# Biases added as sums on GpSimd instead of matmuls, norms applied by ScalarE, presets on GpSimd, loads in pieces, and a new order of steps

## The chip, the cores and the metric

One NeuronCore of a Trainium2 chip runs the kernel alone. The metric is the device time of one launch in microseconds. TensorE (PE), VectorE (DVE), ScalarE (ACT) and GpSimd (POOL) each work through their own instruction list in order; SyncE (SP) only issues DMAs and waits. The engines meet by semaphores.

## The reference, cut to what matters

Four batches of 256 tokens with 128 channels, x, and as many context tokens. Five attention phases with 16 heads of 8 run one after the other, with a norm between them and one MLP after the third:

```
# phase 0: x = x + attend(rope(x Wq + bq), rope(ctx Wk), ctx Wv + bv) Wo + bo
# phase 1: per half h of the tokens (128 each), gates g from c = ctx[:, 0:2]
mod = silu(c) @ ada_w + ada_b        # nine shifts, scales and gates
x_h = x_h + g_msa[h] * mha(mod(ln(x_h)))
# phase 2: the halves attend to each other
x   = x + g_mca * (attend(q_h, k_other, v_other) @ crs_proj_w + crs_proj_b)
x_h = x_h + g_mlp[h] * (gelu(mod(ln(x_h)) @ fc1 + b1) @ fc2 + b2)
# phase 3: x = ln(attend(x, ctx) Wo.T + bo + x) * gamma + beta
# phase 4: x = x + attend(ln(x) * g + b, ctx), weights quantised to three values, + bo
```

## The kernel before, in words

`ORDER` is a written-out list of 1979 two-letter steps (a stream letter and a batch number). `make_steps` turns it into steps (kind, phase p, batch b, index i), and `streams` gives the engine of each stream. Every engine's program is the subsequence of `ORDER` with its steps, so the order is fixed by hand tables; `BANK_OF` gives the PSUM bank of each matmul step and `COUPLED` marks pairs of row steps (max or score) whose matmuls alternate on PE.

One phase of one batch: PE projects k, q and v (L731, L741, in phase 0 L720 and L721). ACT takes q and k with their bias to f32 (L876). POOL splits each into three bf16 parts (L597, L490, L492, L494; in phase 0 partly DVE). SP places each part into `q_stack` and `k_stack` with DMAs (L483), six for q and six for k. Both stacks are preset once per batch by DVE (L945, L946), batch 0's before the loop, the others by step `preset`. In phase 0 the positions are read, turned into row numbers on DVE, and POOL gathers the cosines and sines with indirect DMAs (L569); PE transposes them (L633), ACT takes them (L897), DVE rotates k and q (L991 to L996), and `add_turned` (L501) adds the two halves. PE multiplies the stacks for the row maxima (L662), DVE reduces them (L978), POOL splits the maxima (L507, L508), PE transposes them, ACT or DVE takes them (L900, L513), and SP places them as further rows of `q_stack` (L544). Then PE multiplies the scores with the maximum already subtracted (L663), ACT takes the exp (L844), PE multiplies by v (L705, in phases 1 and 2 L698), and ACT copies the heads out (L894). PE transposes (`unstack`, L633), DVE normalises (L1006, L1007), PE transposes (`heads_t`), ACT adds the bias of v (L903), and PE projects (`out_proj`, L800).

The biases of the output projection are matmuls: two per projection (L789), a column of the identity spread over 128 columns against a row of biases, `rows` in phases 0, 3 and 4, or `gated_bias` (gate times bias, formed by DVE in `take_gate`) in phases 1 and 2. They open the accumulation group that L800 closes. Each f32 matmul is two records in the profile. fc2's bias is made the same way (L816). `add_out` (L1021) adds x on DVE. Norms: DVE takes the statistics (L1030, L1033), POOL forms 1/deviation (L575, L576) and applies the norm (L518, two instructions per batch), PE transposes the result (`norm_t`) and ACT takes it with shift and scale (L914). In phase 3 there are two norms in a row, the first with gamma and beta on POOL (L624, L625).

ACT issues x, the bias rows and three weight groups in five DMAs (`load`; the group q1 to fc2d is one of 1 MB), stores the gates to DRAM and reads them back spread over 128 partitions in one DMA (`spread`, L862). POOL folds a gate into the output weights of phases 1 and 2 (`gate_fold`, L617).

## Time and profile before

| what | us |
|---|---|
| median of 3 runs | 316.98 |
| lowest, highest | 316.63, 322.85 |
| the profiled execution | 320.48 |
| its span | 318.6 |
| PE, DVE, ACT, POOL busy in it | 279.7, 228.2, 216.4, 185.7 |

The span goes from the first to the last instruction of the profiled execution; 1.9 us of its time lie around it. An engine's busy time is the union of its instructions. The chain is followed back from the last instruction, at each step to what released it. PE's instructions overlap each other, so that the busy time of a group can be longer than what it adds to the chain. A DMA's row in the timeline is its issue; its landing is a row of the chain.

### The profile page before, as it was taken

How to read it: one execution, taken by the hardware profiler on the slowest of the kernel's cores; microseconds unless marked ns; L12 is line 12 of the kernel's file. 1: busy time of each engine (PE TensorE's matmuls, PEld its weight loads, DVE VectorE, ACT ScalarE, POOL GpSimd, SP SyncE). 2: the span in 40 equal slices, each digit the busy share in tenths (PEclk: the TensorE clock that was granted, in tenths of full speed). 3: DMA queues.
4: the chain of work that ended last, by engine and by line, in shares of the span. 5: the costliest groups of instructions: out<-in, count | busy, mean ns of one | idle time of the engine just before them, and what ended most of it. 6: DMA issues, size and time to landing. Idle time of an engine off the chain costs nothing.

```text
span 318.6 us, 9133 instructions
## 1 busy us (share of the span) xinstructions
PE 279.7 (88%) x3268; PEld 173.6 (54%) x3268; DVE 228.2 (72%) x473; ACT 216.4 (68%) x462; POOL 185.7 (58%) x349
## 2 busy tenths in 40 slices
PE   2576688999979999988998999899999989999996
PEld 1462344465554666665676686657564546435535
DVE  4898859978872682776472687694979898888733
ACT  1023158668866768667788758898968786788972
POOL 3717414454764668787586759662879787851100
PEclk9977579999995999999999999999999999999999
DMA  4548911421382203333213212220123121220002
GB/s 132 149 110 254 289 24 35 110 59 37 92 245 67 72 26 80 99 84 83 71 45 84 52 52 54 52 69 10 44 61 77 37 67 44 72 74 23 3 3 66
DMA packets 40644, 24.75 MB, mean 78 GB/s; under 512 B 4880, under 2 KB 39576, under 8 KB 40344
## 3 DMA queue, kind: packets, MB, share of 16 engines
q1 hardware_dynamic: 37144, 17.71, 22.0%
q10 hardware_dynamic: 3072, 5.41, 5.2%
q0 software_dynamic: 384, 1.05, 1.1%
q8 instruction: 27, 0.44, 0.6%
q14 instruction: 17, 0.14, 0.2%
HBM read 7.56 MB, written 0.54 MB: 25 GB/s over the span
## 4 chain that ended last, share of the span: by engine, by line
PE 48%; DVE 12%; SPq 10%; DMA 10%; POOL 7%; issue 6%; ACT 5%; ACTq 1%; POOLq 0%; DVEq 0%
PE ps L705 9%; SPq L483 9%; PE ps L663 8%; PE ps L662 8%; PE ps L633 6%; DVE neg_max L978 5%; DMA q_stack<-max_rows_split 4%; PE ps L731 3%; PE ps L698 3%; PE ps L789 3%; DMA q_stack<-q_parts 2%; PE ps L800 2%; DVE k_stack L946 2%; PE ps L819 2%; ACT probs L844 2%
## 5 line engine op out<-in xcount | busy, mean ns | idle before, releaser
L978 DVE TENSOR_REDUCE neg_max<-ps 128x2 f32<-128x512 f32 (+1 forms) x256 | 160.0, 682 | 36.3 <-PE ps L662 35.8
L844 ACT ACTIVATE probs<-ps 128x512 f32<-128x512 f32 x256 | 134.4, 605 | 29.2 <-PE ps L663 26.8
L662 PE MATMUL ps<-k_stack,q_stack 62*128 62x256 bf16 (+1 forms) x640 | 62.9, 259 | 9.8 <-DMA q_stack<-q_parts 5.9
L663 PE MATMUL ps<-q_stack,k_stack 64*128 64x256 bf16 (+1 forms) x640 | 58.8, 254 | 10.2 <-DMA q_stack<-max_rows_split 5.9
L705 PE MATMUL ps<-probs,v_cols 128*32 128x256 f32 x768 | 55.3, 394 | 0.3 <-ACT probs L844 0.2
L662 PEld LDWEIGHTS ps<-k_stack,q_stack 62*128 62x128 bf16 x640 | 28.9, 96 | 39.6 <-issue 10.3
L663 PEld LDWEIGHTS ps<-q_stack,k_stack 64*128 64x128 bf16 x640 | 29.4, 95 | 32.6 <-DMA q_stack<-max_rows_split 8.8
L705 PEld LDWEIGHTS ps<-probs,v_cols 128*32 128x32 f32 x768 | 20.4, 110 | 17.6 <-issue 8.8
L507 POOL CAST max_parts<-neg_max 128x16 bf16<-128x16 f32 (+2 forms) x34 | 6.8, 200 | 39.2 <-DVE neg_max L978 38.7
L876 ACT ACTIVATE q_f<-ps,vec 128x256 f32<-128x256 f32 x32 | 15.0, 476 | 8.2 <-PE ps L731 8.0
L894 ACT ACTIVATE heads_raw<-ps 128x512 f32<-128x512 f32 x20 | 12.0, 600 | 12.6 <-PE ps L705 7.8
L518 POOL TENSOR_SCALAR heads_normed<-x,mean_var,rstd 128x128 f32<-128x128 f32 x24 | 18.9, 798 | 1.3
L698 PE MATMUL ps<-probs,v_cols 128*32 128x128 f32 x512 | 19.1, 277 | 0.0
L1006 DVE RECIPROCAL inv_sum<-ps 128x32 f32<-128x32 f32 x20 | 7.0, 349 | 16.5 <-PE ps L633 16.5
L575 POOL TENSOR_SCALAR var_eps<-mean_var 128x2 f32<-128x2 f32 x20 | 4.6, 228 | 22.0 <-DVE mean_var L1033 21.4
L490 POOL TENSOR_TENSOR q_parts<-q_f,q_parts 128x256 bf16<-128x256 f32 x19 | 12.7, 670 | 6.9 <-ACT q_parts L870 5.9
L731 PE MATMUL ps<-src_t,w 128*128 128x256 f32 x48 | 15.8, 425 | 0.9 <-ACT src_t L914 0.6
L633 PE MATMUL ps<-ident_f,heads_normed 128*128 128x128 f32 x72 | 14.7, 290 | 1.0 <-POOL heads_normed L518 0.3
L576 POOL TENSOR_TENSOR rstd<-var_eps,minus_half 128x2 f32<-128x2 f32 x20 | 14.4, 719 | 1.7
L903 ACT ACTIVATE heads_t_gated<-ps,vec 128x256 f32<-128x256 f32 x20 | 9.2, 472 | 7.9 <-PE ps L633 7.9
L698 PEld LDWEIGHTS ps<-probs,v_cols 128*32 128x32 f32 x512 | 12.6, 109 | 3.1 <-ACT probs L844 1.0
L597 POOL CAST q_parts<-q_f 128x256 bf16<-128x256 f32 x16 | 6.3, 396 | 12.8 <-ACT q_f L876 12.8
(123 smaller groups left out, 451.5 us busy)
## 6 DMA issues: line engine op xcount, KB each, us to landing
k_stack<-k_parts SPq DMA_DIRECT2D x120, 64.0 KB, 2.1
q_stack<-q_parts SPq DMA_DIRECT2D x114, 64.0 KB, 2.1
gates<-gates_dram ACTq DMA_DIRECT2D x1, 1536.0 KB, 7.1
w<-in_w ACTq DMA_DIRECT2D x1, 1024.0 KB, 9.7
rows<-in_rows ACTq DMA_DIRECT2D x1, 704.0 KB, 6.0
q_stack<-max_rows_split SPq DMA_DIRECT2D x44, 4.0 KB
w<-in_w ACTq DMA_DIRECT2D x1, 576.0 KB, 7.1
ctx_t<-in_ctx_t SPq DMA_DIRECT2D x4, 128.0 KB, 2.9
```

Of the source, the lines that this page charges most:

```text
L483: queue.dma_start(stack[slot::ROW_SLOTS, b, :, :], parts_of(kind, b)[part]).then_inc(sem_, 16)
L518: last = ops.tensor_scalar(heads_normed[:, b, qt, :], src[:, b, qt, :], mean_var[:, b, qt, 0:1], rstd[:, b, qt:qt + 1], ALU.subtract, ALU. ...
L576: link(nc.gpsimd.tensor_tensor(rstd[:, b, :], var_eps[:, b, :], minus_half[:, :], ALU.pow))
L633: return nc.tensor.transpose(out, src, by)
L662: return nc.tensor.matmul(out, queries, keys, start=True, stop=True)
L663: return nc.tensor.matmul(out, keys, queries, start=True, stop=True)
L698: last = nc.tensor.matmul(ps[BANKS - 1][32 * j:32 * j + 32, g * T + at * P:g * T + (at + 1) * P], v_cols[:, b, keys_tile(p, at), h, :], pr ...
L705: last = nc.tensor.matmul(ps[BANKS - 1][32 * j:32 * j + 32, g * T:(g + 1) * T], v_cols[:, b, at, h, :], pr[:, at * T:(at + 1) * T], start= ...
L731: last = nc.tensor.matmul(out[:, 0:T], W(f"{kind}{p}"), src[:, b, :], start=True, stop=True)
L844: nc.scalar.activation(probs[:, n % PROB_BUFS, :], ps[bank_of["score", p, b, i]][:, :], ACT.Exp, scale=SCALE).then_inc(of(st), 1)
L876: nc.scalar.activation(f, src, ACT.Identity, bias=V(f"b{letter}{p}")).then_inc(of(st), 1)
L978: nc.vector.tensor_reduce(dst, src, AX.X, ALU.max, negate=True).then_inc(of(st), 1)
```

## The change

The two bias matmuls of every output projection and of fc2 are gone, and each projection is its own accumulation group. POOL forms `base` = x + bias (or x + gate x bias) with a new step `base` per phase and batch and `base_mlp` before the MLP's sum, and DVE's `add_out` and `add_mlp` add `base` instead of x. `gate_fold` now also forms gate x bias, in place for phases 1 and 2 and as `gate_bias` for the MLP, so there are 12 folds instead of 8, the first 8 with two products. The 16 norms that feed `norm_t` are applied by ACT as (1/deviation) x + shift; POOL's new step `deviation` computes the shift with two more small instructions. The presets are on POOL, seen as f32 (half as many elements), batch 0's ahead of the wait for the positions. Seven loads instead of five: the 1 MB group is cut in three. The spread is cut in four, one semaphore per batch. `ORDER` (2028 steps), `BANK_OF` and `COUPLED` are written anew. The ORDER of POOL begins with gathers 1 and 2, then presets 2 and 1. A second copy of the branches `base` and `base_mlp` is never reached and is left out below, as are the tables.

```diff
-APPLY_ON = ("pool", "pool", "pool", "pool")
+PART_ON = ("act", "pool", "pool", "pool", "pool")
+APPLY_ON = ("act", "act", "act", "act")
...
+LOADS = ("x", "rows", 2, 1, 3, 4, 5)
+SPREADS = B
+W_GROUP = (0, 1, 3, 5, 5)
...
-        "Y": ("dve", only([("preset", 0, 0)], not first)),
+        "Y": ("pool", only([("preset", 0, 0)], not first)),
...
-        "p": ("dve", [("apply", p, 1) for p in phases[:-1] if APPLY_ON[p] == "dve"]),
+        "p": ("pool", [("deviation", p, 1) for p in phases[:-1] if APPLY_ON[p] == "act"]),
...
+        "b": ("pool", [("base", p, 0) for p in phases]),
+        "B": ("pool", [("base_mlp", 2, 0)]),
+        "Z": ("pool", [("gate_fold", i, 0) for i in range(3)]),
...
-        "4": ("act", only([("spread", 0, 0), ("spread", 0, 1)], first)),
-        "9": ("act", only([("load", 0, i) for i in range(5)], first)),
+        "4": ("act", only([("keep_gates", 0, 0)] + [("spread", 0, i) for i in range(SPREADS)], first)),
+        "9": ("act", only([("load", 0, i) for i in range(len(LOADS))], first)),
...
-W_GROUPS = (("v0", "o0"), ("q1", "fc2d"), ("ada0", "ada8"), ("q3", "o4"))
+W_GROUPS = (("v0", "o0"), ("q1", "o1"), ("ada0", "ada8"), ("q2", "o2"), ("fc1a", "fc2d"), ("q3", "o4"))
...
+        def preset_stacks(ops, b):
+            ops.memset(q_stack[:, b, :, :].rearrange("p e t -> p (e t)").bitcast(F32), 0.0)
+            return ops.memset(k_stack[:, b, :, :].rearrange("p e t -> p (e t)").bitcast(F32), TWO_ONES)
...
-                link(nc.gpsimd.tensor_tensor(rstd[:, b, :], var_eps[:, b, :], minus_half[:, :], ALU.pow))
+                return nc.gpsimd.tensor_tensor(rstd[:, b, :], var_eps[:, b, :], minus_half[:, :], ALU.pow)
 
             link(nc.gpsimd.memset(minus_half[:, :], -0.5))
             nc.gpsimd.memset(mean_mat[:, :], 1.0 / (D * D)).then_inc(mean_set, 1)
+            clear_v(FIRST[1]).then_inc(first_v_cleared, 1)
+            preset_stacks(nc.gpsimd, FIRST[1]).then_inc(first_preset, 1)
             pool.wait_ge(pos_ready, 1)
             gather(FIRST[1])
-            clear_v(FIRST[1]).then_inc(first_v_cleared, 1)
...
+                elif kind == "preset":
+                    preset_stacks(nc.gpsimd, b).then_inc(of(st), 1)
...
+                    pool.wait_ge(gates_spread[b], 16)
+                    pool.wait_ge(rows_loaded, 16)
+                    if p < 2:
+                        pool.wait_ge(w_loaded[W_GROUP[p + 1]], 16)
+                        pool.wait_ge(*done("rope", 0, b, 0))
+                        link(nc.gpsimd.tensor_tensor(rope_gated_o[:, 2 * b:2 * b + 2, p, :],
+                                                     w[:, W_AT[f"o{p + 1}"]:W_AT[f"o{p + 1}"] + 1, :].broadcast_to([P, NT, D]),
+                                                     gates[:, 2 * b:2 * b + 2, p, :], ALU.mult))
+                        g = gates[:, 2 * b:2 * b + 2, p, :]
+                        nc.gpsimd.tensor_tensor(g, g, row2(f"bo{p + 1}"), ALU.mult).then_inc(of(st), 1)
+                    else:
+                        nc.gpsimd.tensor_tensor(gate_bias[:, 2 * b:2 * b + 2, :], gates[:, 2 * b:2 * b + 2, 2, :],
+                                                row2("bfc2"), ALU.mult).then_inc(of(st), 1)
+                elif kind == "base":
+                    if p == 0:
+                        pool.wait_ge(x_loaded, 16)
+                        pool.wait_ge(rows_loaded, 16)
+                    elif p == 3:
+                        pool.wait_ge(mlp_added, mlp_no(b))
+                    elif p == 4:
+                        pool.wait_ge(*done("apply", 3, b, 0))
+                    else:
+                        pool.wait_ge(*done("add_out", p - 1, b, 0))
+                        pool.wait_ge(*done("gate_fold", p - 1, b, 0))
+                    add = gates[:, 2 * b:2 * b + 2, p - 1, :] if p in (1, 2) else row2({0: "bo0", 3: "bo3", 4: "bo4"}[p])
+                    nc.gpsimd.tensor_tensor(base[:, b, :, :], x[:, b, :, :], add, ALU.add).then_inc(of(st), 1)
+                elif kind == "base_mlp":
+                    pool.wait_ge(*done("add_out", p, b, 0))
+                    pool.wait_ge(*done("gate_fold", 2, b, 0))
+                    nc.gpsimd.tensor_tensor(base[:, b, :, :], x[:, b, :, :], gate_bias[:, 2 * b:2 * b + 2, :], ALU.add
+                                            ).then_inc(of(st), 1)
...
+                    pool.wait_ge(*done("base", p, b, 0))
+                    link(inverse_deviation(p, b, 0))
...
+                elif kind == "deviation":
+                    pool.wait_ge(*done("stats", p, b, int(p == 3)))
+                    nc.gpsimd.tensor_scalar(minus_mean[:, b, :], mean_var[:, b, :, 0], -1.0, None, ALU.mult)
+                    link(inverse_deviation(p, b, int(p == 3)))
+                    nc.gpsimd.tensor_tensor(shift[:, b, :], minus_mean[:, b, :], rstd[:, b, :], ALU.mult).then_inc(of(st), 1)
...
-                    pe.wait_ge(const_loaded, 16)
-                    pe.wait_ge(rows_loaded, 16)
-                    if p in (1, 2):
-                        pe.wait_ge(*done("take_gate", 0, 0, 0))
-                    for qt in range(NT):
-                        nc.tensor.matmul(out[:, qt * D:(qt + 1) * D], *bias_rows(b, qt, p), start=(qt == 0), stop=False,
-                                         skip_group_check=True)
...
-                                                start=False, stop=(qt == NT - 1), skip_group_check=True)
+                                                start=True, stop=True)
...
+                    pe.wait_ge(w_loaded[4], 16)
...
-                        nc.tensor.matmul(out[:, qt * D:(qt + 1) * D], ident[:, 0:1].broadcast_to([P, P]),
-                                         rows[:, R_AT["bfc2"], :], start=True, stop=False)
...
+                    load_w(act, LOADS[i])
+                elif kind == "keep_gates":
                     act.wait_ge(*done("take_gate", 0, 0, 0))
                     act.dma_start(gates_dram.rearrange("(r c) -> r c", r=2 * B),
                                   gates_small[:, :, :].rearrange("r k c -> r (k c)")).then_inc(gates_stored, 16)
...
-                    act.wait_ge(gates_stored, 16)
-                    act.dma_start(gates[:, :, :, :].rearrange("p r k c -> p (r k c)"), gates_dram.partition_broadcast(P)
-                                  ).then_inc(gates_spread, 16)
+                    if i == 0:
+                        act.wait_ge(gates_stored, 16)
+                    n = 2 * 3 * D
+                    act.dma_start(gates[:, 2 * i:2 * i + 2, :, :].rearrange("p r k c -> p (r k c)"),
+                                  gates_dram[n * i:n * (i + 1)].partition_broadcast(P)).then_inc(gates_spread[i], 16)
...
+                elif kind == "apply":
+                    act.wait_ge(*done("deviation", p, b, 1))
+                    src = (heads_t_gated if p == 1 else x)[:, b, :, :]
+                    for qt in range(NT):
+                        last = nc.scalar.activation(heads_normed[:, b, qt, :], src[:, qt, :], ACT.Identity,
+                                                    bias=shift[:, b, qt:qt + 1], scale=rstd[:, b, qt:qt + 1])
+                    last.then_inc(of(st), 1)
...
-            preset_stacks(FIRST[1], first_preset)
...
-                    if p == 0:
-                        dve.wait_ge(x_loaded, 16)
-                    elif p == 3:
-                        dve.wait_ge(mlp_added, mlp_no(b))
-                    elif p == 4:
-                        dve.wait_ge(*done("apply", 3, b, 0))
-                    else:
-                        dve.wait_ge(*done("add_out", 0, b, 0))
+                    dve.wait_ge(*done("base", p, b, 0))
...
-                                            x[:, b, :, :], ALU.add).then_inc(of(st), 1)
+                                            base[:, b, :, :], ALU.add).then_inc(of(st), 1)
...
+                    dve.wait_ge(*done("base_mlp", p, b, 0))
+                    dve.wait_ge(gates_spread[b], 16)
...
-                    nc.vector.tensor_tensor(x[:, b, :, :], product, x[:, b, :, :], ALU.add).then_inc(mlp_added, 1)
+                    nc.vector.tensor_tensor(x[:, b, :, :], product, base[:, b, :, :], ALU.add).then_inc(mlp_added, 1)
...
-                    nc.vector.memset(gated_bias[:, :, :], 0.0)
-                    link(nc.vector.tensor_tensor(gates_small[:, :, :],
-                                                 ps[bank_of["gate", 0, 0, 0]][0:2 * B, 0:3 * D].rearrange("p (a b) -> p a b", a=3),
-                                                 rows[0:2 * B, R_AT["gate1"]:R_AT["gate3"] + 1, :], ALU.add))
-                    nc.vector.tensor_tensor(gated_bias[0:2 * B, :, :], gates_small[:, 0:2, :],
-                                            rows[0:2 * B, R_AT["bo1"]:R_AT["bo2"] + 1, :], ALU.mult).then_inc(of(st), 1)
+                    nc.vector.tensor_tensor(gates_small[:, :, :],
+                                            ps[bank_of["gate", 0, 0, 0]][0:2 * B, 0:3 * D].rearrange("p (a b) -> p a b", a=3),
+                                            rows[0:2 * B, R_AT["gate1"]:R_AT["gate3"] + 1, :], ALU.add).then_inc(of(st), 1)
```

## Rows read from the trace of the kernel before

**Rows 1.** The page: busy time of each engine, share of the span, instructions.
```profile
PE 279.7 (88%) x3268; PEld 173.6 (54%) x3268; DVE 228.2 (72%) x473; ACT 216.4 (68%) x462; POOL 185.7 (58%) x349
```

**Rows 2.** The chain that ended last: shares by engine (the page), by line (the chain).
```profile
PE 48%; DVE 12%; SPq 10%; DMA 10%; POOL 7%; issue 6%; ACT 5%; ACTq 1%; POOLq 0%; DVEq 0%
...
by line: PE ps L705 9.1%; SPq L483 8.8%; PE ps L663 8.5%; PE ps L662 8.5%; PE ps L633 6.4%; issue 5.5%; DVE neg_max L978 5.4%; DMA q_stack<-max_rows_split 4.2%; PE ps L731 3.1%; PE ps L698 2.9%; PE ps L789 2.6%; DMA q_stack<-q_parts 2.2%; P
```

**Rows 3.** The page: TensorE's granted clock in 40 slices of 7.97 us.
```profile
PEclk9977579999995999999999999999999999999999
```

**Rows 4.** Timeline, 0 to 36 us: start, duration, engine, line, operation [idle before, releaser].
```profile
5.76 1.30 POOL L569 DMA_INDIRECT rope_gated_o<-in_rope,pos_row  x1 [4.68 <-DVE pos_row L954]
...
11.37 0.60 ACT L897 ACTIVATE rope_hidden<-ps 128x512 f32<-128x512 f32 x1 [6.97 <-PE ps L633]
...
14.62 1.76 DVE L946 MEMSET k_stack<- 128x2048 bf16 x1 [0.38 <-issue]
...
16.30 0.36 DVE L995 TENSOR_TENSOR q_f<-ps,rope_hidden 128x256 f32<-128x256 f32 x1
...
24.97 0.57 ACTq L849 DMA_DIRECT2D x<-in_x  x1
...
26.42 0.61 PE L662 MATMUL ps<-k_stack,q_stack 62*128 62x256 bf16 x6 [3.12 <-DMA q_stack<-q_parts]
```

**Rows 5.** Groups by line and form: count, busy us, mean ns, idle before.
```profile
L518 POOL TENSOR_SCALAR heads_normed<-x,mean_var,rstd 128x128 f32<-128x128 f32 x24 | 18.9, 798 | 1.3
...
L518 POOL TENSOR_SCALAR heads_normed<-heads_t_gated,mean_var,rstd 128x128 f32<-128x128 f32 x16 | 12.6, 798 | 0.8
...
L914 ACT ACTIVATE src_t<-ps,mods 128x128 f32<-128x128 f32 x24 | 9.8, 464 | 1.5 <-PE ps L633 1.4
...
L946 DVE MEMSET k_stack<- 128x2048 bf16 x4 | 7.1, 1765 | 1.5 <-issue 1.5
...
L617 POOL TENSOR_TENSOR rope_gated_o<-w,gates 128x256 f32<-128x256 f32 x8 | 5.8, 727 | 0.1
...
L575 POOL TENSOR_SCALAR var_eps<-mean_var 128x2 f32<-128x2 f32 x20 | 4.6, 228 | 22.0 <-DVE mean_var L1033 21.4 <-POOL q_parts L494 0.2
...
L561 POOL MEMSET v_cols<- 128x1024 f32 x4 | 3.8, 954 | 0.1
...
L945 DVE MEMSET q_stack<- 128x1024 uint32 x4 | 3.6, 912 | 0.6 <-issue 0.6
...
L564 POOL MEMSET v_cols<- 128x128 f32 x8 | 1.4, 204 | 0.2
```

**Rows 6.** Groups by line and form: the bias matmuls on TensorE.
```profile
L789 PE MATMUL ps<-rows,ident_f 128*128 128x128 f32 x48 | 8.1, 292 | 0.6 <-ACT heads_t_gated L903 0.6
...
L789 PE MATMUL ps<-gated_bias,ident_f 128*128 128x128 f32 x32 | 5.5, 294 | 0.3 <-ACT heads_t_gated L903 0.3
...
L816 PE MATMUL ps<-rows,ident_f 128*128 128x128 f32 x16 | 3.2, 281 | 0.0
```

**Rows 7.** The chain, 300 to 318.6 us: start, duration, what.
```profile
313.24 0.45 PE ps L789 x4
```

**Rows 8.** The chain at three max placements, and the page on the spread.
```profile
34.97 4.83 DMA q_stack<-max_rows_split
...
89.05 5.11 DMA q_stack<-max_rows_split
...
215.54 1.78 DMA q_stack<-max_rows_split
...
gates<-gates_dram ACTq DMA_DIRECT2D x1, 1536.0 KB, 7.1
```

**Rows 9.** The chain, 40 to 80 us: the fourth preset and take_gate.
```profile
55.45 1.76 DVE k_stack L946
...
73.17 0.77 DVE gated_bias L1058
```

**Rows 10.** The waits: engine, line, waited for: us in all, times, longest.
```profile
POOL var_eps L575 <- DVE mean_var L1033: 21.4, 12, 6.9
```

## What I expect of the change, and why

> **What bounds the kernel now.** I read the busy line first, then the slices, the chain, and last the stretches where the chain leaves TensorE. Busy: PE 279.7 us of a 318.6 us span, DVE 228.2, ACT 216.4, POOL 185.7 [rows 1]. TensorE is the nearest to a bound, but the chain that ended last lies on PE for only 48%: 12% is DVE, 10% SP's issuing, 10% DMA, 7% POOL, 5% ACT [rows 2]. So microseconds taken from PE count where the chain is on PE, and the rest must come from the waits. The clock row shows three places that are not steady: slices 3, 4 and 6 at 0.7, slice 5 (31.9 to 39.8 us) at 0.5, and slice 13 (95.6 to 103.5) at 0.5, i.e. 1.2 GHz instead of 2.4 [rows 3]. Everywhere else it is 0.9 or more. Each of the 0.5 slices holds or follows a long landing of a row-max placement [rows 8]. The three kinds of place where the change acts are thus: the start, two DMA stalls, and the bias matmuls spread over the whole.
>
> **1. Presets leave DVE.** Four pairs of memsets (L945, L946), 0.91 + 1.77 us each, 10.7 us of DVE in all [rows 5]. At the start, batch 0's cos/sin are in SBUF when L897 ends, 11.37 + 0.60 = 11.97 us. DVE is then still in presets, the last of which (L946 at 14.62) ends at 16.4, and the rotation of k (L995) begins at 16.30 [rows 4]. Without presets on DVE it begins at about 12.0: 4.3 us earlier. What follows down to the first max matmul at 26.42 [rows 4] is the same ladder of small DVE steps and placements (the new order has the same ones in nearly the same order, one turn later for batch 1), so it should come at about 22. The fourth pair lies in the chain at 54 to 57: 1.76 + 0.91 and the gap between them, 3.0 us [rows 9]. On POOL the pair is two memsets over 1024 f32 (the bitcast halves the element count): the row for that shape is 0.954 us, 1.9 a pair, 7.6 for all [rows 5]. For batch 0, v_cols (0.95 + 2 x 0.2) and the pair now stand ahead of the first gather, which started at 5.76 after 4.68 us in which POOL only waited for positions [rows 4]: POOL is free from 1.1 us, and 3.3 us of memsets [rows 5] end at about 4.5. They are covered; if POOL's own gaps use that up, the gather comes up to 0.5 us late and the whole start with it. The presets of batches 1 and 2 stand behind two gathers each of 2.6 us (each gather is two DMAs of 1.3 us; the presets end at about 17), in time for placements of batch 1 after 20. Terms: -4.3 (range -2 to -5) and -3.0 (0 to -3.0).
>
> **2. Bias matmuls go.** 20 output projections lose two f32 matmuls each (four records) and fc2 loses two for each of four batches: L789 8.1 + 5.5 us and L816 3.2 us of PE busy, 16.8 in all [rows 6]. That is busy time of pipelined instructions. In the tail, where projections stand back to back, a bias step advances the chain by 0.45 us [rows 7]. So 24 x 0.45 = 10.8 us of PE are freed. The chain itself has 2.6% of 318.6 = 8.3 us on L789 [rows 2]. Off the chain the freed time only becomes idle. I take -8 (range -3 to -10.8); the last four steps, 1.8 us in the tail, are certain.
> The Trainium skill ("Perfetto Trace Analysis", Identifying the Most-Contended Engine) says that matmul busy share is a poor measure because the instructions are pipelined. This trace agrees: 16.8 us busy against 10.8 advanced; by the busy figure the sum would be 6 us lower.
>
> **3. Sums, folds and norms.** POOL gets 20 base sums, 4 base_mlp and 12 more gate products of 128x256 f32, by the nearest row 0.727 each [rows 5]: 36 x 0.727 = 26.2. Deviation adds two 128x2 ops of 0.228 at 16 places: 7.3. Presets 7.6. It loses the 32 applies of i = 1 (of 24 + 16) at 0.798: 25.5 [rows 5]. Net +15.5, POOL at 201 us. The phases themselves are neutral (+0.73 + 0.46 - 1.6 = -0.4 per norm); the growth is presets and folds, most of it early, where POOL has room. POOL turns 22 of its 186 us into chain (7%) [rows 1, 2], 12%; I take +1.9 (0 to +8). The sum over x (base) is queued before its projection, needs only the previous residual, and lies under that phase's scores; if it were late, DVE's add_out and with it the bank would wait 0.7 us each. DVE's waits at add_out are the same count. take_gate loses a memset and a product, of which 0.77 is on the chain [rows 9]: -1.0 (0 to -1).
> ACT gets 32 applies of 128x128 with bias and scale from SBUF: nearest row L914, 9.8 / 24 = 0.41 [rows 5], 13.1 us (7 to 15), and five more DMA issues of 0.57 [rows 4], 2.9. ACT goes to about 232 us, still under PE's 263. In its queue the exps stand behind each apply, and PE's score banks wait for exps. ACT turns 16 of 216 us into chain (5%), 7%; but these sit behind a new wait (for deviation), so I take a quarter of 16: +4.0 (+1 to +16). Chain of one norm, L576 aside, which stays: 0.23 + 1.6 before, 3 x 0.23 + 0.8 and one more hop after: equal, 0.
>
> **4. Loads in pieces.** At 34.97 and 89.05 the placement of row maxima (4 KB) lands after 4.83 and 5.11 us; the same placement takes 1.78 at 215.54 [rows 8]. The first follows x, rows and two groups of weights, issued on ACT's queue from 24.97 on at about 0.6 us each [rows 4]; the second follows the gate spread, 1536 KB in one DMA that lands in 7.1 us [rows 8]. Now the spread goes in four parts of 384 KB and the big group in three, fc and phase 3 weights much later. Excess: 3.05 and 3.3 us. The first keeps most of its bytes in front (x, rows, ada stay), the second loses three quarters of them. I take the second, -3.3 (0 to -6.4), and nothing for the first. The clock of slice 13 fell right after this second pause: a gain on top that I don't count.
>
> **Sum.** -4.3 - 3.0 - 8.0 - 1.0 - 3.3 + 4.0 + 1.9 = -13.7 us against the profiled execution (320.5 us, span 318.6), so 306.8 there. The median of the runs is 317.0, 3.5 below it; scaled, -13.5: I predict 303.5 us. A change within 2% (310.6 to 323.3) is about what a measurement of this kernel cannot tell from none. The order of all steps is new as well, with the same number of exps and maxima ahead of each projection, 181 coupled row steps against 177, and the same nine switches between exp and gelu: no term for it, but it is what can move every term.
>
> **Rivals.**
> A. *The forecast*, 298 to 308: chance 0.47.
> B. *Everything lands*: all 10.8 of PE, both stalls (6.4), no ACT cost, and a clock that doesn't fall in slice 13. -4.3 - 3.0 - 10.8 - 1.0 - 6.4 + 1.9 = -23.6, about 293.5. For it: PE busy in nearly all slices. Against: 52% of the chain is elsewhere. Chance 0.11 (292 to 298).
> C. *Pieces change nothing in the landings, and DVE hides its presets*: the bytes are the same and the DMA engines are shared, the placement still waits 5 us behind them, and the fourth preset was hidden. -13.7 + 3.3 + 3.0 = -7.4, about 309.5 (308 to 311). For it: stall one keeps its bytes. Chance 0.17. The Trainium skill ("DMA: Bandwidth & Descriptors", Issuing engines are not separate DMA queues) says that DMAs of all engines interleave on the same 16 engines; by it alone only fewer bytes in front of a placement help, and the first landing here, on another queue than the loads, agrees.
> D. *The bound moves on*: DMA issue on SP (10% of the chain) and POOL's splits fill the freed time, only start and tail are left: -4.3 - 1.8 - 1.0 + 1.9 = -5.2 or less, 312 (311 to 317). For it: 0.6 us issues stand in the chain for 8.8% [rows 2]. Chance 0.18.
> E. *Slower: ACT parks behind POOL.* The apply waits in ACT's queue for deviation. POOL itself waited for statistics 21.4 us in 12 waits, 1.8 each [rows 10]. If ACT stands as long at each of 16 applies, with exps behind it, that is +28.5 in place of +4.0: 303.5 + 24.5 = 328. From 1.1 us each the gain is gone, from 1.5 it is over 2% slower. Against: a queue order can put exps ahead of the apply, and ACT has 32% of slack. Chance 0.07 (over 317), half of it over 323.
>
> Faster by over 2%: A, B and C but for their edge, 0.73; within 2%: 0.23; slower: 0.04. The range 295 to 312 leaves out E, most of D and the lower half of B.
>
> **What would show it.** Right: L995's counterpart at about 12 us and the first max at about 22; no memset on DVE; PE busy near 263; the landing after the first gate spread under 2.5 us; no 0.5 in slice 13; tail from last value matmul to the end 1.5 to 2 us shorter. Wrong: a gather after 6.2 us; ACT waits on deviation of over 15 us in all; exps' waits up while PE is idle between; POOL over 90% busy in the last third, with base late. If PE's busy falls by 16 and its idle time rises by as much, D is the case.

## The result, and the profile after

| kernel | median us | ratio to the kernel before | 95% interval |
|---|---|---|---|
| before | 319.15 | 1 | |
| changed | 303.63 | 0.9531 | 0.9427 to 0.9635 |
| predicted | 303.5 (295 to 312) | | |

Over all occasions on which it ran, the kernel before scatters from 316.4 to 328.7 us between its executions and the changed one from 299.2 to 304.2, so a ratio is known to about one per cent and no better. On two later occasions the changed kernel ran again beside others, at 300.6 and 301.2 us (ratios 0.9345 and 0.9448). Both kernels have a slower state, over 1.5% above the fastest execution, in some executions; ratios and intervals leave those out, medians keep them. The profiled execution went from a span of 318.6 to 302.1 us.

The page of the changed kernel (busy time, TensorE's granted clock in 40 slices, and the chain's shares by engine) answers [rows 1 to 3]:

```profile
PE 269.0 (89%) x3172; PEld 164.6 (54%) x3172; DVE 215.8 (71%) x463; ACT 225.0 (74%) x494; POOL 199.2 (66%) x393
...
PEclk9968799999999799799789999999999999999998
...
PE 60%; DMA 9%; DVE 8%; ACT 7%; POOL 6%; issue 6%; SPq 4%; ACTq 0%; POOLq 0%; DVEq 0%
```

In this execution the chain was on TensorE for 60% of 302.1 us (181 us), against 48% of 318.6 (153 us) before. One profile isn't enough for such a share. In the two later profiles of the same kernel it is 51% of 297.9 (152 us), whose line is below, and 54% of 298.5 (161 us):

```profile
PE 51%; POOL 12%; DMA 8%; DVE 8%; issue 7%; ACT 6%; SPq 6%; ACTq 0%; POOLq 0%
```

What all three show is less time of the chain elsewhere: 166 us before, and 121, 146 and 137 us now. SP's issuing went from 10% to 4, 6 and 4%, DVE from 12% to 8% in all three. GpSimd has 6, 12 and 11%, against 7% before. So the kernel got shorter because the chain spends less time off TensorE; whether it spends more on it differs from execution to execution.

The start in the timeline (start, duration, engine, line, operation, what ended the idle time), against [rows 4]:

```profile
2.32 0.95 POOL L506 MEMSET q_stack<- 128x1024 f32 x1
...
3.21 0.95 POOL L507 MEMSET k_stack<- 128x1024 f32 x1
...
5.97 1.31 POOL L581 DMA_INDIRECT rope_gated_o<-in_rope,pos_row  x1 [1.81 <-DVE pos_row L1020]
...
12.05 0.42 DVE L1060 TENSOR_TENSOR q_f<-ps,rope_hidden 128x256 f32<-128x256 f32 x1 [6.39 <-ACT rope_hidden L960]
...
23.52 0.98 PE L726 MATMUL ps<-k_stack,q_stack 62*128 62x256 bf16 x8 [1.41 <-DVE heads_normed L1061]
...
35.40 0.60 ACT L900 ACTIVATE probs<-ps 128x512 f32<-128x512 f32 x1 [0.78 <-PE ps L727]
```

GpSimd's presets end at 4.2 us, and it still waits 1.81 us for the positions; the rotation begins at 12.05 instead of 16.30; the first max (its matmuls) comes at 23.52 instead of 26.42 and the first exp at 35.40 instead of 40.49.

What was added, in the groups by line and form (count, busy us, mean ns, idle before), against [rows 5]:

```profile
L998 ACT ACTIVATE heads_normed<-x,shift,rstd 128x128 f32<-128x128 f32 x24 | 10.5, 484 | 1.6 <-POOL shift L692 1.6
...
L654 POOL TENSOR_TENSOR base<-x,rows 128x256 f32<-128x256 f32 x12 | 8.5, 725 | 0.7 <-DVE x L1099 0.7
...
L638 POOL TENSOR_TENSOR gates<-gates,rows 128x256 f32<-128x256 f32 x8 | 5.8, 725 | 0.6
...
L690 POOL TENSOR_SCALAR minus_mean<-mean_var 128x2 f32<-128x2 f32 x16 | 3.9, 242 | 14.6 <-DVE mean_var L1089 14.3
...
L506 POOL MEMSET q_stack<- 128x1024 f32 x4 | 3.9, 962 | 0.1
```

And a stall that the kernel before did not have, in the timeline from 140 us:

```profile
140.41 1.37 SPq L556 DMA_DIRECT2D q_stack<-max_rows  x2
...
140.42 0.34 ACTq L472 DMA_DIRECT2D w<-in_w  x1
...
140.80 0.45 ACTq L472 DMA_DIRECT2D w<-in_w  x1
```

in the chain of waits (start, duration, what):

```profile
141.13 5.07 DMA q_stack<-max_rows
```

and in the windows around it (length, then busy us and instructions of PE, PEld, DVE, ACT and POOL, granted clock, DMA share, GB/s):

```profile
140.00:147.00 7.00, 2.62 (x33) 1.95 (x32) 1.85 (x7) 1.76 (x4) 6.30 (x12) 0.99 0.58 186
147.00:153.00 6.00, 5.79 (x68) 3.89 (x66) 3.22 (x9) 3.73 (x9) 1.22 (x3) 0.50 0.00 0
```

Two weight loads of 512 KB are issued in the same microsecond as a placement of row maxima (8 KB). The placement lands after 5.07 us, TensorE is busy for 2.62 of 7 us, and it then runs at a granted clock of 0.50, the 1.2 GHz level, for the next six. The stall of [rows 8] at 89 us is gone, and this one has taken its place.

### The profile page after: what moved, and what is told of

Same layout as the page of the kernel before. It is cut to its first block, busy times and chain, and to the rows that moved or that the text cites. A ratio compares the mean times of both kernels' runs of the same rounds, so it can differ in the third digit from the quotient of the medians.

```text
span 302.1 us, 9011 instructions
## 1 busy us (share of the span) xinstructions
PE 269.0 (89%) x3172; PEld 164.6 (54%) x3172; DVE 215.8 (71%) x463; ACT 225.0 (74%) x494; POOL 199.2 (66%) x393
## 4 chain that ended last, share of the span: by engine, by line
PE 60%; DMA 9%; DVE 8%; ACT 7%; POOL 6%; issue 6%; SPq 4%; ACTq 0%; POOLq 0%; DVEq 0%
PE ps L769 11%; PE ps L726 11%; PE ps L727 9%; PE ps L697 9%; PE ps L795 4%; DVE neg_max L1043 4%; PE ps L857 3%; PE ps L762 3%; ACT probs L900 3%; DMA q_stack<-q_parts 3%; PE ps L875 3%; SPq L491 2%; PE ps L805 2%; DMA q_stack<-max_rows 2%; PE ps L868 1%
## 5 line engine op out<-in xcount | busy, mean ns | idle before, releaser
L727 PE MATMUL ps<-q_stack,k_stack 64*128 64x256 bf16 (+1 forms) x640 | 60.2, 253 | 4.9 <-DMA q_stack<-max_rows 3.6
L769 PE MATMUL ps<-probs,v_cols 128*32 128x256 f32 x768 | 53.5, 386 | 0.5 <-ACT probs L900 0.5
L726 PEld LDWEIGHTS ps<-k_stack,q_stack 62*128 62x128 bf16 x640 | 30.7, 97 | 33.2 <-issue 10.7
L762 PE MATMUL ps<-probs,v_cols 128*32 128x128 f32 x512 | 20.3, 286 | 0.6 <-ACT probs L900 0.6
L1077 DVE TENSOR_TENSOR x<-ps,base 128x256 f32<-128x256 f32 x12 | 5.0, 422 | 15.4 <-PE ps L857 15.1
L502 POOL TENSOR_TENSOR q_parts<-split_r,q_parts 128x256 bf16<-128x256 f32 x19 | 12.7, 670 | 1.5
L498 POOL TENSOR_TENSOR k_parts<-q_f,k_parts 128x256 bf16<-128x256 f32 x18 | 12.1, 670 | 2.4 <-ACT k_parts L928 1.6
L697 PE MATMUL ps<-ident_f,heads_raw 128*128 128x128 f32 x80 | 13.3, 290 | 0.5 <-ACT heads_raw L957 0.5
L690 POOL TENSOR_SCALAR minus_mean<-mean_var 128x2 f32<-128x2 f32 x16 | 3.9, 242 | 14.6 <-DVE mean_var L1089 14.3
```

The costliest lines, as they stand in the source:

```text
L498: ops.tensor_tensor(part[1], full, part[0], ALU.subtract).then_inc(of(step), 1)
L502: ops.tensor_tensor(part[2], rest, part[1], ALU.subtract).then_inc(of(step), 1)
L697: return nc.tensor.transpose(out, src, by)
L726: return nc.tensor.matmul(out, queries, keys, start=True, stop=True)
L727: return nc.tensor.matmul(out, keys, queries, start=True, stop=True)
L762: last = nc.tensor.matmul(ps[BANKS - 1][32 * j:32 * j + 32, g * T + at * P:g * T + (at + 1) * P], v_cols[:, b, keys_tile(p, at), h, :], pr ...
```

## The experiments

Each is the changed kernel with one thing altered (4, 5 and 6 alter several), beside the kernel before on the same chip. Ratios are to the kernel before. Runs 1 to 3 had the first yardstick on their chip, runs 5, 6 and the second of 9 the other; runs 4, 7, 8 and the first of 9 had none, and are set against the three ratios of the changed kernel.

**The yardsticks.** The changed kernel ran twice more, with no edit.

> The changed kernel unchanged, as the yardstick on this chip for the other runs of the call. Every theory: 0.953 of the kernel before, about 303.6 us, within 1%.

> The changed kernel unchanged, the yardstick of this call. Every theory: 0.935 to 0.953 of the kernel before, about 300 to 304 us.

Measured: 300.56 us, 0.9345 (0.9254 to 0.9436), and 301.24 us, 0.9448 (0.9367 to 0.9529). TensorE's busy time was 263.4 and 263.2 us in their profiles, against 269.0 in the one above, at a mean clock of 0.971 and 0.976 against 0.952.

**1. Presets back on VectorE.**

```diff
-        "Y": ("pool", only([("preset", 0, 0)], not first)),
+        "Y": ("dve", only([("preset", 0, 0)], not first)),
...
-            preset_stacks(nc.gpsimd, FIRST[1]).then_inc(first_preset, 1)
...
+            preset_dve(FIRST[1]).then_inc(first_preset, 1)
```

> The changed kernel, with all four preset pairs back on VectorE in the order that the kernel before has them (batch 0's before the loop, the others at their place in the new order, bf16 as before). Theory (the presets on VectorE held up the start by 4.3 us and lay in the chain with 3.0 us later): 5 to 7 us slower than the changed kernel, the first rotation of k no earlier than 14 us, against 12.05 now. Rival (VectorE has slack, the presets are hidden, or only the place in the order matters): less than 2 us slower.

Measured: 311.37 us, 0.9642 (0.9537 to 0.9747), 10.8 us slower than the yardstick of the same chip. The rotation still began at 11.96 us: batch 0's preset was over before the rotation could start, and the two others stand behind the first rotations in the new order. They hit the splits instead. The timeline (same columns as above):

```profile
17.48 0.91 DVE L1012 MEMSET q_stack<- 128x1024 uint32 x1 [0.16 <-issue]
18.77 1.76 DVE L1013 MEMSET k_stack<- 128x2048 bf16 x1 [0.38 <-issue]
...
20.70 0.91 DVE L1012 MEMSET q_stack<- 128x1024 uint32 x1 [0.16 <-issue]
...
21.99 1.76 DVE L1013 MEMSET k_stack<- 128x2048 bf16 x1 [0.38 <-issue]
...
29.16 1.19 PE L723 MATMUL ps<-k_stack,q_stack 62*128 62x256 bf16 x8 [8.96 <-DVE heads_normed L1063]
```

The first max came at 29.16 us after TensorE had stood for 8.96 us; in the changed kernel's profile above, at 23.52 after 1.41, and in the yardstick's from the same chip at 21.64 after 2.12. So 7.5 of the 10.8 us are there. Presets on VectorE do hold the start, by more than was expected, though not at the rotation: what was expected of the place was wrong, of the mechanism right. The edit brings back two things together, the engine and the bf16 form of k_stack's preset (1.76 us, where q_stack's 32-bit form takes 0.91 for the same bytes). What 32-bit presets on VectorE would cost was not run.

**2. The bias matmuls back, the sums kept.**

```diff
                 elif kind == "out_proj":
+                    for qt in range(NT):
+                        nc.tensor.matmul(out[:, qt * D:(qt + 1) * D], ident[:, 0:1].broadcast_to([P, P]), zero_row[:, :],
+                                         start=(qt == 0), stop=False, skip_group_check=True)
...
                 elif kind == "fc2":
...
+                        nc.tensor.matmul(out[:, qt * D:(qt + 1) * D], ident[:, 0:1].broadcast_to([P, P]), zero_row[:, :],
+                                         start=True, stop=False)
```

> The changed kernel, with the two bias matmuls of every output projection and of fc2 put back on TensorE at their old places in the program, with a row of zeros, while the sums on GpSimd stay: the pure price of 48 f32 matmuls. Theory: 8 us slower than the changed kernel (3 to 10.8), TensorE busy up by 16 us. Rival (the freed time was idle time anyway, the bound is on the other engines): under 3 us slower, with TensorE's idle time falling by as much as its busy time grows.

Measured: 310.78 us, 0.9611 (0.9516 to 0.9705), 10.2 us slower. TensorE was busy 278.5 us at a mean granted clock of 0.949, 15.1 more than in the yardstick (263.4 at 0.971), but only 9.5 more than in the first profile (269.0 at 0.952), whose clock is nearer. The groups of the zero-row matmuls:

```profile
L852 PE MATMUL ps<-zero_row,ident_f 128*128 128x128 f32 x80 | 14.1, 301 | 1.5 <-ACT heads_t_gated L974 1.4
...
L880 PE MATMUL ps<-zero_row,ident_f 128*128 128x128 f32 x16 | 3.3, 290 | 0.2 <-ACT rope_hidden L999 0.2
```

That is 17.4 us of busy time, for steps that advance a chain by 0.45 us each, 10.8 in all [rows 7]. Nearly all of the 10.8 came back as time. In the new order TensorE's freed time is not idle.

**3. Norms applied on GpSimd.**

```diff
                 elif kind == "deviation":
-                    nc.gpsimd.tensor_scalar(minus_mean[:, b, :], mean_var[:, b, :, 0], -1.0, None, ALU.mult)
                     link(inverse_deviation(p, b, int(p == 3)))
-                    nc.gpsimd.tensor_tensor(shift[:, b, :], minus_mean[:, b, :], rstd[:, b, :], ALU.mult).then_inc(of(st), 1)
+                    apply_norm(nc.gpsimd, b, heads_t_gated if p == 1 else x).then_inc(of(st), 1)
...
-                    act.wait_ge(*done("deviation", p, b, 1))
-                    src = (heads_t_gated if p == 1 else x)[:, b, :, :]
-                    for qt in range(NT):
-                        last = nc.scalar.activation(heads_normed[:, b, qt, :], src[:, qt, :], ACT.Identity,
-                                                    bias=shift[:, b, qt:qt + 1], scale=rstd[:, b, qt:qt + 1])
```

> The changed kernel, with the 16 norms that feed the transposes applied by GpSimd again, at the place of the deviation step; ScalarE's 32 activations and the two small deviation steps are gone. Theory of the prediction (ScalarE pays 4 us for the applies and issues, GpSimd 1.9 for all its extra work; undoing saves ScalarE 13 us and loads GpSimd with 18): within 3 us either way, ScalarE about 211 us busy, GpSimd about 217. Rival (GpSimd is the engine that is short in this order): 4 us or more slower, with the waits for parts and for the maxima's split growing.

Measured: 310.04 us, 0.9588 (0.9494 to 0.9682), 9.5 us slower: the rival. The page, of this run's execution of 314.42 us (mean granted clock 0.929): busy time, the chain's shares by engine, and by line:

```profile
PE 274.0 (88%) x3172; PEld 166.6 (53%) x3172; DVE 216.1 (69%) x463; ACT 214.5 (69%) x462; POOL 217.6 (70%) x393
...
PE 38%; POOL 20%; DVE 13%; DMA 10%; issue 8%; SPq 7%; ACT 3%; POOLq 0%; ACTq 0%; DVEq 0%
PE ps L768 8%; PE ps L725 7%; DVE neg_max L1037 7%; DMA q_stack<-q_parts 6%; PE ps L696 6%; PE ps L726 5%; SPq L491 5%; POOL heads_normed L530 5%; PE ps L794 3%; PE ps L761 2%; POOL rstd L588 2%; PE ps L856 2%; PE ps L874 2%; POOL q_parts L498 2%; SPq L556 1%
```

GpSimd at 70% busy is on the chain for 20% of the span, where the changed kernel has it at 66 or 67% busy and, in its three profiles, 6, 12 and 11% of the chain. An engine that is far from full can still be the one that holds the chain. Added up along the chain, the applies (L530) stand in it for 15 us, against 1.6 in each profile of the changed kernel, and the splits of q and k, which stand in GpSimd's queue behind them, for 26 us against 7. This chain is of one execution, the longest of the four; the 9.5 us are between the medians.

**4. All parts in the old order.** The three tables `ORDER`, `BANK_OF` and `COUPLED` are those of the kernel before, with the new steps set in by a rule: presets after gather 2, each base before its normalise and after its fold, deviation in the apply's old place, ScalarE's apply right before norm_t, the third fold and base_mlp after add_out of phase 2. First lines of `ORDER`:

```diff
-    "K0K1I1Q0R0z0r0D0r0k0K2D010R1y0z1r1q0D1Q300k1I2Y2R2Y1E0y010E0Q1r1Q2W1y110J2D10000I311y1z2r2r2d2901111q121d2q2W2w2"
...
+    "K0R0z0r0Q0r0K1I1R1z1D0D0k0Q1q0I2Y2Y110R2z2r1y0E0r100I300E000y0W01010D1D1k19090Q2W190K2r2d2r2J1y1909090M0M0M0m0m0"
...
```

> All parts of the change (sums on GpSimd, norms on ScalarE, presets on GpSimd, loads and spread in pieces), but with the order, bank and coupling tables of the kernel before; the new steps are put in by rule: a preset after the gather, the sum ahead of the normalisation of its phase, the apply ahead of its transpose, the three loads together at the fourth load's place, the four spreads together at the second spread's. Theory of the prediction (no term for the order): within 3 us of the changed kernel. Rival (the new order earns a good part of the gain, because each part has its own best place): 5 us or more slower than the changed kernel, though faster than the kernel before.

Measured: 331.31 us, 1.0335 (1.0235 to 1.0435): slower than the kernel before, though every part is in. The waits of TensorE, in its execution of 335.27 us, name one cause (engine, tile, line, what it waited for: us, times, longest):

```profile
PE ps L697 <- ACT heads_normed L998: 18.5, 14, 1.7
```

and in the changed kernel the same row is

```profile
PE ps L697 <- ACT heads_normed L998: 1.0, 2, 0.9
```

The transposes waited for an apply that stood in ScalarE's queue, where the rule puts it right ahead of them; the apply itself waited for GpSimd's shift for only 0.5 us in all. That is a bad place that my rule chose, so the next run takes it away.

**5. The same, norms on GpSimd.** The edits of 3 and 4 together. On top of 4:

```diff
-                    nc.gpsimd.tensor_tensor(shift[:, b, :], minus_mean[:, b, :], rstd[:, b, :], ALU.mult).then_inc(of(st), 1)
+                    apply_norm(nc.gpsimd, b, heads_t_gated if p == 1 else x).then_inc(of(st), 1)
```

> The old order with the new parts by rule, as in the earlier run, but with the norms applied by GpSimd, so that no transpose waits for an apply in ScalarE's queue (18.5 us of TensorE's waits there). If the bad place of the apply was the whole loss: below the kernel before by 4% or so, near 305 us. If the old order cannot use any of the parts: still 315 us or more. In between, the difference to the changed kernel with the apply on GpSimd (310.0) is the worth of the order alone.

Measured: 321.47 us, 1.0103 (1.0023 to 1.0182), the kernel before being at 321.05. Without the waits for the apply, presets off VectorE, no bias matmuls and smaller loads bring nothing in the old order, where my rule puts them. The applies on ScalarE cost 2.3% there (1.0103 against 1.0335) and save 2.4% in the new order (0.9588 against 0.9345).

This run also settles a question on the loads. The spread is in four parts, but issued together (81.14 to 83.27 us), and the placement of row maxima behind them still lands late, as in the kernel before (5.11 us at 89.05):

```profile
84.59 5.09 DMA q_stack<-max_rows_split
```

In run 4 the same placement takes 6.29 us. So cutting the spread in pieces does not remove that stall by itself.

**6. The new order with the old parts.** Edits 1, 2 and 3, the one-piece spread of 7, and no sums (the edit of 8) together. The bias is left out of the result. The seven loads stay.

```diff
+        "Y": ("dve", only([("preset", 0, 0)], not first)),
...
+                    apply_norm(nc.gpsimd, b, heads_t_gated if p == 1 else x).then_inc(of(st), 1)
...
+                        nc.tensor.matmul(out[:, qt * D:(qt + 1) * D], ident[:, 0:1].broadcast_to([P, P]), zero_row[:, :],
...
-                    nc.gpsimd.tensor_tensor(base[:, b, :, :], x[:, b, :, :], add, ALU.add).then_inc(of(st), 1)
```

> The new order with the old parts: presets on VectorE, norms applied on GpSimd, 48 bias matmuls on TensorE (of a row of zeros), no sums or bias products on GpSimd, the spread in one DMA. The bias is left out of the result, its work is there. If the parts bring what they brought one at a time (10.8 + 10.2 + 9.5 us, less what the sums cost GpSimd) and add up: 325 us or more, slower than the kernel before. If the order brings the gain and the parts share one gain among them: 308 to 315 us.

Measured: 326.7 us, 1.0253 (1.019 to 1.0316), against 301.24 for the changed kernel beside it: 25.5 us. One at a time the parts were worth 10.8 + 10.2 + 9.5 = 30.5 us; so in the new order they nearly add up. This kernel has no sums on GpSimd, so their cost is not in the 25.5.

**7. The gate spread in one DMA.**

```diff
                         act.wait_ge(gates_stored, 16)
-                    n = 2 * 3 * D
-                    act.dma_start(gates[:, 2 * i:2 * i + 2, :, :].rearrange("p r k c -> p (r k c)"),
-                                  gates_dram[n * i:n * (i + 1)].partition_broadcast(P)).then_inc(gates_spread[i], 16)
+                        act.dma_start(gates[:, :, :, :].rearrange("p r k c -> p (r k c)"),
+                                      gates_dram.partition_broadcast(P)).then_inc(gates_spread[0], 16)
```

> The changed kernel with the gate spread in one DMA of 1536 KB at the place of the first of the four. Theory (the single spread stood in front of a placement of row maxima, 3.3 us): 2 to 5 us slower, with a landing of 4 us or more between 64 and 75 us. Rival (the bytes are the same, and at this place of the new order nothing urgent is behind them): within 1.5 us of the changed kernel.

Measured: 303.95 us, 0.9491 (0.9409 to 0.9573), inside the span of the changed kernel's three ratios, so no difference that these runs resolve. Its chain has this row:

```profile
65.17 8.77 DMA gates<-gates_dram
```

One spread lands after 8.77 us, where the four land after 3.8 to 5.2 each, and the chain does wait for it (the first fold needs it). It did not delay a placement of row maxima: the next one is issued only at 73.76 us. Whether that is worth one or two microseconds stays open.

**8. No sums and no bias products on GpSimd.** The biases of the output projections and of fc2 are left out of the computation.

```diff
-                    nc.gpsimd.tensor_tensor(base[:, b, :, :], x[:, b, :, :], add, ALU.add).then_inc(of(st), 1)
...
-                        nc.gpsimd.tensor_tensor(g, g, row2(f"bo{p + 1}"), ALU.mult).then_inc(of(st), 1)
...
-                                            base[:, b, :, :], ALU.add).then_inc(of(st), 1)
+                                            x[:, b, :, :], ALU.add).then_inc(of(st), 1)
```

> The changed kernel without any bias in the output projections and fc2: the 24 sums and the 12 bias products on GpSimd are left out (36 instructions of 0.73 us, 26 us of GpSimd), and VectorE adds x as before. Theory of the prediction (GpSimd turns 12% of its work into the chain): 2 to 4 us faster than the changed kernel. Rival (GpSimd is the engine that is short): 6 us or more faster. A third: equal, because the sums lie where GpSimd waits anyway.

Measured: 301.17 us, 0.9412 (0.9323 to 0.95), again among the changed kernel's own ratios. 25.6 us of GpSimd's work went (busy 174.5 instead of 200.1), and its wait for the statistics grew from 14.3 us to this:

```profile
POOL minus_mean L652 <- DVE mean_var L1058: 25.1, 12, 7.1
```

A good part of the sums, 11 of 26 us by this row, lies where GpSimd would wait anyway. 18 us more of applies cost 9.5 us (run 3), and 26 us of sums no more than these runs resolve: 1 us by the mean of the changed kernel's three ratios (0.9441), some 4 at the edge of the intervals. What I take from it, that the work differs in whether something waits behind it, fits the chain of run 3.

**9. The two late loads moved away from the placement.**

In `ORDER`, the two steps written `90` that stood side by side, at 901 and 902 of 2028, now stand at 230 and 281, where the trace has about 48 and 54 us:

```diff
-    "V0h0U3t3229090U0n0U3U0t0S1S1S1e1S1S1M2b0o3x3p3S1U0o0e1V1e1V1M2M2M2m2e1V1m2m2x0v3m2V1e1S1S1e1e1e1N3u3M2m2M2M2m2m2"
...
+    "31S1S1e1S1M290i3M2m2m2e1U0t0S1e1S1S1U0V1V1e1e1e1S1S1e1e1S1S1b0o0x0e1e1M2m2M2m213V1V1j3j3M2S1S1m2M2m2G0e1M2S1p0S1"
+    "M2902323s2e1e1T2g0V123M2M2M2C2m2m2m2m2M2V1e1V1v0b2m2N0u0V1h1G013m2W032g0M2w0S2e2S2b3m2b1s2e2M3U140Q0q070K0T2C232"
...
```

> The changed kernel with the two 512 KB weight loads, which ScalarE now issues at 140.4 us in the same moment as a placement of row maxima that then lands after 5.07 us, moved to about 48 and 54 us. Theory (a load in front of an urgent placement costs its landing and the slower clock after it): 3 to 6 us faster than the changed kernel, TensorE's busy share between 140 and 147 us back above 0.8 and no stretch at the 1.2 GHz level behind it. Rival (another placement near 50 us waits instead, or the placement at 140 is slow for another reason): within 1.5 us.

> The changed kernel with the two late weight loads moved to about 48 and 54 us, a second time beside the changed kernel on one chip. Theory: 3 to 6 us faster than the changed kernel of the same call. Rival (the difference between calls was that of the chips): within 1.5 us.

Measured: 298.01 us, 0.9256 (0.9136 to 0.9376), and 298.15 us, 0.9347 (0.9264 to 0.9429), the second beside 301.24 for the changed kernel on the same chip (0.9448). The windows of the changed kernel in its last run:

```profile
136.00:142.00 6.00, 4.26 (x78) 3.07 (x68) 2.94 (x10) 3.19 (x7) 4.81 (x9) 1.00 0.61 164
142.00:148.00 6.00, 3.65 (x48) 3.00 (x48) 0.56 (x2) 3.10 (x7) 3.48 (x8) 0.72 0.27 93
```

and of this kernel beside it:

```profile
136.00:142.00 6.00, 4.99 (x94) 3.74 (x90) 3.30 (x9) 3.49 (x8) 4.08 (x8) 1.00 0.27 70
142.00:148.00 6.00, 5.32 (x115) 3.99 (x118) 3.95 (x13) 5.55 (x12) 5.18 (x11) 1.00 0.05 14
```

The stall and the low clock behind it are gone: TensorE waits for that placement for 0.31 us, where it waited for 3.37 in the first profile. Another transfer into q_stack, near the loads' new place, now takes 2.86 us (its row in the chain):

```profile
48.88 2.86 DMA q_stack<-max_rows_split
```

The profiled spans are 298.5 and 295.7. This is the fastest kernel of the study, by about 3 us or 1%; the intervals of the two ratios overlap, and on the first yardstick's chip the changed kernel itself had 0.9345. So the sign rests on two measurements and on the trace together, and the size is at the low end of what was expected.

## Why the prediction was right, and where its steps were not

The total was 303.5 against 303.63. It is right in that TensorE's matmuls and the start gained, and in the size, but two of its terms were too small, one had the wrong sign, and the order had no term. They cancelled: part of the closeness is luck, and on two later occasions the same kernel took 300.6 and 301.2 us.

- **Presets, -7.3.** The start moved as told: rotation at 12.05 (12.0 told), gather not late, first max at 23.52, in the yardsticks' profiles from about 22 (22 told). Undoing it costs 10.8 in the new order. The term was too small for that order, because I counted only DVE's own time; TensorE also stood for 8.96 us before the first max. Not told either: in the two yardsticks' profiles the chain of the first 25 us runs over GpSimd, through the gathers and the presets of batches 2 and 1 (3.6 us), so the presets are not covered there.
- **Bias matmuls, -8.0 (3 to 10.8).** Undoing them costs 10.2, close to the upper bound, 24 x 0.45. I had cut the sum to what lay on the chain of the kernel before (8.3 us). That chain had 52% elsewhere, and that share was 40, 49 and 46% in the profiles of the changed kernel. PE busy "near 263" was 269.0 in the profile shown and 263.4 and 263.2 in the others: busy time of matmuls moves with the granted clock. The Trainium skill ("Perfetto Trace Analysis", Identifying the Most-Contended Engine) calls the busy share of matmuls a poor measure of how close a kernel is to roofline for another reason: pipelined instructions look smaller in the trace. Run 2 agrees that it is a poor measure, but here the group looks larger, 17.4 us busy for some 10 us of time.
- **ScalarE, +4.0.** The step that failed. The price of an instruction was right (10.5 / 24 = 0.44 us against 0.41 told, ACT 225.0 against about 232 told), but I priced the receiving engine and called the giving one nearly neutral. Run 3 shows 9.5 us gained by taking 1.6 us of apply out of GpSimd's queue per norm. The term for the norms should have been about -9 in the new order; in the old order, with my rule, the same step costs 2.3%.
- **GpSimd, +1.9 (0 to 8).** Busy 199.2 against 201 told. The sums cost no more than runs resolve, 1 us by the mean and some 4 at most (run 8).
- **Loads, -3.3.** The stall at 89 us went, as told, and the clock of slice 13 with it. But the cause was not the smaller pieces: in the old order the four pieces leave a landing of 5.09 and 6.29 us (runs 5 and 4), and in the new order one piece of 1536 KB brings no such stall (run 7). In the new order the next placement of maxima is issued at 72.29 us, 8 us after the first piece (64.47). And a stall of the same kind came at 141 us, 5.07 us long, and the clock fell behind that one. I had written "fc and phase 3 weights much later" and not asked what they would meet there. No run puts the 1 MB load back as one, so the net of this term is not shown; run 9 shows about 3 us lost at the place of the two late loads. The Trainium skill ("DMA: Bandwidth & Descriptors", Issuing engines are not separate DMA queues) says that DMAs started by ScalarE, SyncE or GpSimd run on the same 16 DMA engines and interleave. The trace agrees: with 1 MB issued from ScalarE's queue beside it, a placement from SP's landed after 5.07 us, and with the loads moved away it did not (run 9).
- **No term for the order.** This hid the most. The two orders and the two sets of parts, each cell with its ratio:

| | old parts | new parts |
|---|---|---|
| old order | 1 | 1.010 (norms on GpSimd), 1.034 (on ScalarE) |
| new order | 1.025 | 0.9345 to 0.9531 |

The cell for the new order with the old parts keeps the seven loads. Neither the parts nor the order gains anything alone. The order by itself costs about 2.5% (ratio 1.0253), and the parts' gain in it is 25 us and adds up nearly part by part; in the old order it is nothing. The caution: my rule for putting the new steps into the old order is one of many, and a better one might gain; and the new order was written for the new parts. Which pieces of the order matter was not tested.
- **Rivals.** E (ScalarE parks behind deviation) was priced at +28.5; the row is 2.2 us in 5 waits:

```profile
ACT heads_normed L998 <- POOL shift L692: 2.2, 5, 0.6
```

In the old order its mirror image came true, TensorE waiting 18.5 us for the apply. D (the gain is swallowed) is like what happened in the old order; whether by SP's issuing and the splits, as D has it, no run tests. C's half about the loads was right: pieces alone change nothing in the landing (runs 4 and 5), and a stall stayed, at another place. In the tail the chain on TensorE after the last value matmul ended at 295.29 and the span at 302.1, 6.8 us, against 310.39 and 318.6, 8.2 us: 1.4 us shorter, just under the 1.5 to 2 told.

## What to carry to other kernels

When work moves between engines that each run a fixed list, price what stands behind it in the list it leaves, not only its cost in the list it joins: 18 us of work on an engine at 66% was worth 9.5 us, 26 us on the same engine nothing that these runs resolve. A change of parts and a change of order can be worth nothing each and 5 to 7% together, so an experiment that undoes one part in the final order measures that part only for that order. After a bulk load is moved, look up what small urgent transfer is issued in its first microseconds at the new place.

## What the runs showed of the hardware that I had not expected

- A placement of 8 KB, issued by SP, lands after 4.7 to 5.3 us in the changed kernel's three profiles and those of runs 2, 7 and 8, where ScalarE issues two loads of 512 KB beside it. In the first of them TensorE's granted clock is 0.50 for the six microseconds after the pause (2.62 us busy in 7).
- GpSimd sets 128x1024 f32 in 0.96 us, nearly as fast as VectorE's 0.91 for 128x1024 uint32 (the same bytes), and much faster than VectorE's 1.77 for the 128x2048 bf16 of k_stack, which are the same bytes too.
- GpSimd's two-input add of 128x256 f32 takes 0.725 us, less than its 0.80 for a scale and shift of half as many elements (128x128) with two values per partition; ScalarE does the latter in 0.48.
